# A graph network's second message layer: scattered rows kept in SBUF or sent through DRAM, twenty or twenty-six batches gathered beside a copy

## What is computed

```python
deg = maximum(segment_sum(ones, dst), 1)            # per node
s = deg ** -0.5
h = relu(layernorm(x))
x = x + s * segment_sum((s * h)[dst] * edge_weight, src)          # layer 0
h = relu(layernorm(x))
x_i, x_j = h[dst], h[src]
feat = concat([x_i, x_j - x_i])                                    # 512 wide
msg = relu(feat @ W1 + b1) @ W2 + b2                               # 512 -> 512 -> 256
x = x + segment_sum(msg, dst) / (segment_sum(ones, dst) + 1e-8)    # layer 1
```

## Time and profile before

| | |
|---|---|
| median of 3 timed runs | 2128.58 us (2127.1 to 2130.37) |
| the profiled execution | 2115.95 us, span of its core 2114.1 us |
| mean granted TensorE clock | 0.914 |
| busy, share of the span | TensorE 80%, VectorE 69%, ScalarE 48%, GpSimd 60% |
| DMA | 376.43 MB |

### The profile page before, as it was taken

One profiled execution on the slowest core, in us unless ns is written; L12 is line 12 of the kernel. 1 busy time (PEld: TensorE's weight loads), 2 busy tenths in 40 slices (PEclk: granted clock), 3 DMA queues, 4 the chain that ended last, 5 costly groups with the idle time before them and its releaser, 6 DMA issues.

```text
span 2114.1 us, 45720 instructions
## 1 busy us (share of the span) xinstructions
PE 1692.6 (80%) x13740; PEld 1478.0 (70%) x13740; DVE 1465.7 (69%) x5883; ACT 1009.9 (48%) x2064; POOL 1261.7 (60%) x1004
## 2 busy tenths in 40 slices
PE   4958888887676676620599999999999999999991
PEld 1238877776576566620488889888888888888881
DVE  6969989897677666720477777777767767677660
ACT  0014445443333333310376666767666656666561
POOL 2023323268888878865443433378888888888854
PEclk9979999998888888865799999999999999999996
DMA  7989999856565565545999999955555555555543
GB/s 242 318 295 336 323 334 326 270 103 107 99 109 103 98 105 101 102 50 94 335 326 333 342 336 339 336 114 97 95 94 92 97 94 97 92 97 94 95 65 39
DMA packets 140468, 376.43 MB, mean 178 GB/s; under 512 B 31392, under 2 KB 95657, under 8 KB 127529
## 3 DMA queue, kind: packets, MB, share of 16 engines
q0 software_dynamic: 84672, 128.51, 33.9%
q1 hardware_dynamic: 27452, 208.63, 27.4%
q10 hardware_dynamic: 28304, 38.85, 7.0%
HBM read 323.36 MB, written 258.12 MB: 275 GB/s over the span
## 4 chain that ended last, share of the span: by engine, by line
POOL 21%; PE 18%; issue 11%; DMA 3%; ACT 0%; DVE 0%; ACTq 0%; POOLq 0%; DVEq 0%
POOL table_out L937 11%; POOL ends L925 10%; PE ps_h L1249 10%; PE ps_m L1263 5%; DMA table_out<-e_ring,e_targets_all 2%; PE ps_t L1236 2%; PE ps_s L1276 2%; ACT ends L1148 0%; DMA ends<-x,keys 0%; DVE e_moments L999 0%; ACT hid L1162 0%; DVE out_sum L1071 0%; ACTq L1133 0%; POOLq L935 0%; DVE out_lo L1076 0%
## 5 line engine op out<-in xcount | busy, mean ns | idle before, releaser
L925 POOL DMA_INDIRECT ends<-x,keys x392 | 399.3, 1019 | 306.9 <-PE ps_h L1249 109.0
L774 PE MATMUL ps_deg<-table,hot 128*128 128x128 bf16 x5488 | 352.9, 226 | 80.4 <-issue 72.6
L774 PEld LDWEIGHTS ps_deg<-table,hot 128*128 128x128 bf16 x5488 | 328.7, 101 | 99.7 <-issue 91.0
L467 POOL DMA_INDIRECT x<-sums_ring,targets_all x196 | 323.4, 1650 | 89.0 <-issue 63.5
L937 POOL DMA_INDIRECT table_out<-e_ring,e_targets_all x196 | 319.9, 1632 | 92.2 <-issue 55.9
L457 POOL DMA_INDIRECT rows<-in_x,row_idx x196 | 205.1, 1046 | 240.9 <-ACT normed L702 188.3
L1249 PE MATMUL ps_h<-feat_hi,w_hi 128*128 128x512 f32 x784 | 314.2, 401 | 9.4 <-DVE feat_lo L1066 4.8
L1249 PE MATMUL ps_h<-feat_lo,w_hi 128*128 128x512 f32 x784 | 310.4, 396 | 0.0
L1249 PE MATMUL ps_h<-feat_hi,w_lo 128*128 128x512 f32 x784 | 310.3, 396 | 0.0
L788 PE MATMUL ps_sum<-msg_hi,same 128*128 128x260 f32 x784 | 151.0, 322 | 137.7 <-issue 131.2
L1263 PE MATMUL ps_m<-w_hi,hid_hi 128*128 128x256 f32 x784 | 227.9, 291 | 9.8 <-DVE hid_lo L1061 8.3
(11 more groups left out here) (141 smaller groups left out, 3447.2 us busy)
## 6 DMA issues: line engine op xcount, KB each, us to landing
table_out<-x SPq DMA_DIRECT2D x400, 252.0 KB
x<-in_x SPq DMA_DIRECT2D x400, 250.0 KB
hi_row<-hi_rows ACTq DMA_DIRECT2D x49, 256.0 KB
src_row<-src_rows ACTq DMA_DIRECT2D x49, 256.0 KB
dst_row<-dst_rows ACTq DMA_DIRECT2D x49, 256.0 KB
ends<-x,keys POOLq DMA_INDIRECT x392
rows<-in_x,row_idx POOLq DMA_INDIRECT x196
x<-sums_ring,targets_all POOLq DMA_INDIRECT x196
```

Of the source, the lines that this page charges most:

```text
L467: pool.indirect_dma_start(out=x1_d, out_offset=bass.IndirectOffsetOnAxis(ap=targets_all[:, b, j:j + 1], axis=0), in_=sums_ring[:, b % RING ...
L774: last = nc.tensor.matmul(ps_deg[q][k][:, j * P:(j + 1) * P], hot[:, c, k, j * P:(j + 1) * P], table[:, c, part, :], start=(c == 0 and par ...
L925: pool.indirect_dma_start(out=ends[b % NE][:, n, :], out_offset=None, in_=x1_d, in_offset=bass.IndirectOffsetOnAxis(ap=keys[:, 1 - end, at ...
```

## The change

`e_ring` goes. ScalarE's `scale` writes into one of two tiles `e_sums`, and a new `keep(b, q)` at the end of ScalarE's step writes the batch, half a megabyte, to `sums_d` in DRAM. SP, once it has issued the copy, reads the batches back in order into six tiles `back`, and `scatter` reads from those; `e_in_ring` is now `e_scaled`, and `e_ring_free` is `back_free`, for which SP waits and not ScalarE. The space goes to the gathers: NE is 10 and LEAD1 is 26. The pace of the lead is a new one: its batches 2 to 25 are spread over TensorE's steps 0 to 15. After the copy 9/4 gathers go with each half batch. The loops of the three compute engines are written out.

```diff
     RING0 = 26
-    RING1 = 20
-    NE = 4
+    BACK = 6
+    NE = 10
     LEAD0 = 24
-    LEAD1 = 20
+    LEAD1 = 26
+    sums_d = nc.dram_tensor("sums_d", (NB, P, W * D), fp32).ap()
...
-            e_ring = sb("e_ring", [P, RING1, W, D], fp32)
+            e_sums = [sb(f"e_sums{q}", [P, W, D], fp32) for q in range(2)]
+            back = [sb(f"back{k}", [P, W, D], fp32) for k in range(BACK)]
...
# SyncE, behind the copy
+                for b in range(NB):
+                    sp.wait_ge(kept[b % 2], 16 * (b // 2 + 1))
+                    if b >= BACK:
+                        sp.wait_ge(back_free, b - BACK + 1)
+                    sp.dma_start(back[b % BACK][:].rearrange("p j d -> p (j d)"), sums_d[b, :, :])\
+                        .then_inc(back_in[b % BACK], 16)
...
# GpSimd, scatter and scatter_end
-                    pool.wait_ge(e_in_ring, GROUPS * (b + 1) + g + 1)
                     if g == 0:
+                        pool.wait_ge(back_in[b % BACK], 16 * (b // BACK + 1))
                         pool.wait_ge(e_target_ready, b + 1)
...
-                            in_=e_ring[:, b % RING1, j, :], in_offset=None, compute_op=ALU.add)\
+                            in_=back[b % BACK][:, j, :], in_offset=None, compute_op=ALU.add)\
...
-                        pool.sem_inc(e_ring_free, 1)
+                        pool.sem_inc(back_free, 1)
...
# GpSimd, pace
+                STEPS = 4 * (LEAD1 - NE)
+                PAIRS = W * (LEAD1 - 2)
...
-                    elif b >= 3:
-                        if n < 4:
-                            pool.wait_ge(mm1_done, KH * (b - 3) + 2 + n)
-                        else:
-                            pool.wait_ge(mm2_done, GROUPS * (b - 3) + n // 2 - 1)
+                    elif b >= 2:
+                        step = (W * (b - 2) + n // 2) * STEPS // PAIRS
+                        c, k = step // 4, step % 4
+                        if k < 2:
+                            pool.wait_ge(mm1_done, KH * c + 2 * k + 2)
+                        else:
+                            pool.wait_ge(mm2_done, GROUPS * c + k - 1)
...
-                    for n in range(min(left, 11 * c // 4), min(left, 11 * (c + 1) // 4)):
+                    for n in range(min(left, 9 * c // 4), min(left, 9 * (c + 1) // 4)):
...
# ScalarE
+                def keep(b, q):
+                    act.wait_ge(e_scaled, GROUPS * (b + 2))
+                    act.dma_start(sums_d[bass.ds(b, 1), :, :].rearrange("o p w -> (o p) w"),
+                                  e_sums[q][:].rearrange("p j d -> p (j d)")).then_inc(kept[q], 16)
+
+                def scale(b, t, q, g):
                     act.wait_ge(e_summed, GROUPS * (b + 1) + g + 1)
-                    act.wait_ge(e_ring_free, b + 1)
+                    if g == 0 and not (isinstance(b, int) and b < 2):
+                        act.wait_ge(kept[q], 16 * t)
...
+                    if not first(b):
+                        keep(b - 1, 1 - q)
                     if load:
                         load_keys(b + 2, q)
...
# the three compute engines
-                step(*whole(0))
-                with act.Fori(0, QUADS) as i:
-                    for n in range(1, NE + 1):
-                        step(NE * i + n, 2 * i + n // 2, n % 2, n % NE, i + n // NE)
-                for b in range(NE * QUADS + 1, NB):
+                for b in range(NB):
                     step(*whole(b), last=b == NB - 1, load=b < NB - 2)
```

More of the change, by code:

```diff
@@ L882, in gnn_preln_two_layers @@
             e_summed = sem("e_summed")
-            e_in_ring = sem("e_in_ring")
-            e_ring_free = sem("e_ring_free")
+            e_scaled = sem("e_scaled")
+            kept = [sem(f"kept{q}") for q in range(2)]
+            back_in = [sem(f"back_in{k}") for k in range(BACK)]
+            back_free = sem("back_free")
             e_scattered = sem("e_scattered")
@@ L952, in pace @@
                         pool.wait_ge(ends_in[0], 16 * 2 * W)
[L953 to L957, removed]
-                        else:
-                            pool.wait_ge(mm1_done, 1)
-                    elif b >= 3:
-                        if n < 4:
-                            pool.wait_ge(mm1_done, KH * (b - 3) + 2 + n)
-                        else:
-                            pool.wait_ge(mm2_done, GROUPS * (b - 3) + n // 2 - 1)
+                    elif b == 2 and n == 0:
+                        pool.wait_ge(ends_in[1], 16 * 2 * W)
+                    elif b >= 2:
[3 more added lines that the diff above has]
+                            pool.wait_ge(mm1_done, KH * c + 2 * k + 2)
+                        else:
+                            pool.wait_ge(mm2_done, GROUPS * c + k - 1)
                 for b in range(LEAD1):
@@ L1040, in after_of @@
                     dve.wait_ge(e_deg_done, b + 1)
-                    dve.wait_ge(e_in_ring, GROUPS * b)
+                    dve.wait_ge(e_scaled, GROUPS * b)
                     nc.vector.reciprocal(inv_deg[q][:], deg_eps[:]).then_inc(inv_deg_done, 1)
@@ L1127, in _ @@
                 act.sem_inc(e_normed_done, 2)
-                act.sem_inc(e_in_ring, GROUPS)
+                act.sem_inc(e_scaled, GROUPS)
                 def load_keys(b, q):
@@ L1170, in out_high @@
                                          ACT.Copy).then_inc(out_hi_done, 1)
-                def scale(b, q, g):
+                def keep(b, q):
[3 more added lines that the diff above has]
+                def scale(b, t, q, g):
                     act.wait_ge(e_summed, GROUPS * (b + 1) + g + 1)
-                    act.wait_ge(e_ring_free, b + 1)
+                    if g == 0 and not (isinstance(b, int) and b < 2):
+                        act.wait_ge(kept[q], 16 * t)
                     act.wait_ge(inv_deg_done, b + 1)
-                    act.sem_inc(waited, 1)
                     for a in range(G):
                         j = G * g + a
-                        last = nc.scalar.activation(e_ring[:, bass.ds(b % RING1, 1), j, :], ps_s[g][:, a * D:(a + 1) * D],
+                        last = nc.scalar.activation(e_sums[q][:, j, :], ps_s[g][:, a * D:(a + 1) * D],
                                                     ACT.Copy, scale=inv_deg[q][:, j:j + 1])
-                    last.then_inc(e_in_ring, 1)
+                    last.then_inc(e_scaled, 1)
                 def step(b, t, q, u, v, last=False, load=True):
@@ L1202, in step @@
                         if not first(b):
-                            scale(b - 1, 1 - q, g)
+                            scale(b - 1, t - 1 + q, 1 - q, g)
                         out_high(b, g)
+                    if not first(b):
+                        keep(b - 1, 1 - q)
                     if load:
@@ L1213, in _ @@
                     feat_high(0, k)
-                step(*whole(0))
-                with act.Fori(0, QUADS) as i:
-                    for n in range(1, NE + 1):
-                        step(NE * i + n, 2 * i + n // 2, n % 2, n % NE, i + n // NE)
-                for b in range(NE * QUADS + 1, NB):
+                for b in range(NB):
                     step(*whole(b), last=b == NB - 1, load=b < NB - 2)
                 for g in range(GROUPS):
-                    scale(NB - 1, (NB - 1) % 2, g)
+                    scale(NB - 1, (NB - 1) // 2, (NB - 1) % 2, g)
+                keep(NB - 1, (NB - 1) % 2)
             @block.tensor
@@ L1270, in sums @@
                         pe.wait_ge(out_lo_done, GROUPS * b + g + 1)
-                        pe.wait_ge(e_in_ring, GROUPS * b + g + 1)
+                        pe.wait_ge(e_scaled, GROUPS * b + g + 1)
                         for a in range(G):
```

3 lines of the change are left out of this document (removed).

## The result

The changed kernel takes 2142.73 us (median of 12 runs, 2134.51 to 2146.03), the kernel before 2127.84 us in the same sessions: ratio 1.0068, 95% interval 1.0056 to 1.0080. It is slower by 15 us; the forecast was 12.4 us slower. The profiled execution has a span of 2138.9 us.

A forecast was written before the change was run, and what follows sets the result against it. GpSimd's scatters and gathers bound the kernel: first scatter at 1435.5, plus 576 with gathers, 109 without and 6, gave a 2126.5 us span, 12.4 more than before, so 2141 timed; range 2107 to 2175.

The forecast's parts named there:

- What sets the end: Layer 1: GpSimd's scatters and gathers set the end; TensorE keeps 34 us in hand.
- The copy's end: Layer 1 during the copy: added traffic lengthens it by 52 us (bounds 27 and 64); first scatter 50 us later.
- The gathers' share: During the copy: 53 more gathers, 6.9 MB at 3.5 us per MB; with row loads 27 us.
- The writes': During the copy: writing 9.2 MB of kept sums to DRAM adds 26 to 37 us.
- Rival A: During the copy: added traffic is cheap, 27 us not 52, giving 2116; faster if under 35 us; chance 0.29.
- The rhythm: After the copy: groups with gathers take 7.05 us each (bounds 6.92 and 7.4), 81.75 groups making 576 us.
- Rival B: After the copy: scatters wait for reads and writes, 7.4 and 7.5 us a group, giving 2183; chance 0.10.
- Groups without gathers: Last scatters: 6.7 us a group instead of 6.28 (bounds 6.28 and 7.5), 16.25 groups making 109 us.
- The sum: Whole kernel: 1435.5 + 576 + 109 + 6 = 2126.5 us of span, 12.4 more than before; 2141 timed.
- The small terms: Extra DMA issue, buffers, tiles, unrolled loops and a start effect: covered; unrolling gives at most 0.4 us per iteration.
- Batch 2's late gathers: Layer 1's start: VectorE waits for them, so TensorE loses some 10 us once, with 34 us still in hand.
- That TensorE stays at 20.47 us: Layer 1: TensorE's batches keep 20.47 us each, with one gap of about 10 us in step 0.

The follow-up runs named there:

- the repeat: The changed kernel itself run again, on the third chip beside three others; ratio 1.0066 to the kernel before.
- DRAM alone: Changed kernel with 20 batches beside the copy, 4 ends tiles, old pace and 11/4 gathers a group, keeping the messages' way through DRAM; ratio 1.0215.
- reads alone: Changed kernel without writes to DRAM; SP reads as many bytes from x1 instead; ratio 0.9864 on the second chip, 0.9937 on the third.
- the halves: Changed kernel with every write and read cut in two of 0.26 MB, same bytes; ratio 1.0014 on the second chip, 1.0080 on the third.
- no trip: Changed kernel without the messages' write to DRAM and read back, scatters adding zeros; ratio 0.9908, and 0.9890 in the second session.
- loops out: Kernel before with the loops of the three compute engines written out, nothing else changed; ratio 1.0011.
- six ends: Two kernels: the one before, loops written out, 16 ring places, 6 ends tiles, 22 batches ahead; ratio 0.9926 with 5/2 gathers a group, 1.0015 with 11/4.
- writes alone: Changed kernel with the writes to DRAM but without SP's reads, scatters adding zeros; ratio 0.9988.
- the four repeats: Third-chip reruns: changed kernel 1.0066, without DRAM writes and reads 0.9890, with reads only (from x1) 0.9937, with transfers cut in two 1.0080.

## Why the prediction was right, and its sizes

**What sets the end.** Right. GpSimd's chain of scatters does, before and after; TensorE's last sums stand 53 us ahead of the last scatter.

**The copy's end.** The mechanism was right: GpSimd stands for 40 us, the engines are at 0.98 until then. The term was 50 us and measured 41.5 (44.4 in the repeat). The gathers' share was right on the first chip, where it was measured alone: 21.7 us for 48 gathers, 6.3 MB, which at my 3.5 us per MB are 22. The writes' was the one that was mis-sized. I priced a written MB at 2.8 to 4.0 us, like rows of other queues; 9 MB cost 12.6 to 16.3 us on the first chip, and on the third 14.6 by the last copy DMA, not 26 to 37. The 3 us for the first read back are borne out: from the last copy DMA to the first scatter pass 8.8 and 10.2 us with the trip, 5.9 and 5.8 without. Rival A was nearer on the price of a write, but the whole stayed above its point of decision (35 us).

**The rhythm.** I took 7.05 and it was 7.23: 82 groups make this 15 us. I had split it as 6.92 undisturbed and 0.13 for the trip. The undisturbed one is 7.11 and 7.12 in two kernels without a trip; the trip adds 0.11. So the trip's part was right and the price of the shorter groups was too low: late landings, nearly absent behind 2.75 gathers (0.3 us in all in the earlier trace rows), come to light behind two, mostly beside a row load, and the gathers themselves took 3% longer. The trace of before had the size, and I took one row of it: in layer 0 the scatter behind two gathers starts after 0.58 us in that row, but after 0.66 on average in all 20 such places, seven of them above 0.7 and one at 1.41, and after 0.30 in the 20 behind three (a group scatters four tiles there). With those 0.36 us in three groups of four the sum would have been 6.88 + 0.27 = 7.15. That the trip adds so little is not general either: in the kernel with DRAM alone it added 0.29 a group (7.81 against 7.52), though more gathers stand between; why stays open. Rival B did not decide: two-gather groups took 7.04 and 7.00 us on average, under the 7.2 that I had named as the limit.

**Groups without gathers.** 6.7 expected, 6.65 measured, 6.36 and 6.43 without the trip.

**The sum.** The first scatter 8 us less, the time after the copy 14 us more (a saving of 23, not 37): +18.6 in the profiles where the sum had 12.4, and +14.9 in the timed runs. The terms missed by 8 us one way and 14 the other. That the total came within 3 us in timed runs is in part luck; the direction and the chain that sets it are not.

**The small terms.** The loops cost nothing that shows (1.0011, interval with 1). Batch 2's late gathers did stall TensorE. VectorE waits for them and comes late to its next work, and TensorE waits for that ahead of step 1's products:

```profile
1062.05 1.40 DVE L1008 BATCH_NORM_STATS2 e_moments<-ends 128x6 f32<-128x256 f32 x4 [9.21 <-DMA ends<-x,keys]
1065.97 0.79 PE L1259 MATMUL ps_h<-feat_hi,w_hi 128*128 128x512 f32 x1 [6.12 <-DVE feat_lo L1075]
```

Step 1 starts 64.5 us behind layer 1's start, 58.7 before: 6 us, not 10, and covered as forecast, since the last sums follow the last gather (2024.6) by 50 us as before. That TensorE stays at 20.47 us was wrong: its batches in the changed kernel are some 21.3 us apart beside the copy. The chain that ended last, two of its products:

```profile
1108.96 11.44 PE ps_h L1259 x48
...
1130.35 11.29 PE ps_h L1259 x48
```

With that, 0.8 us in each of 19 steps, it still was not the end.

**Where the gain went.** Moving 48 gathers ahead of the copy's end is worth 20 to 23 us by the ratios (0.9908 on the first chip, 0.9890 on the third) and 17 to 22 by the medians (2109.11 against 2125.68, 2105.5 against 2127.66). The trip that makes room for them costs 37 us. The change does what it says and pays more for the space than the space brings.

## What to carry to other kernels

Space bought by a trip through DRAM is paid with DMA time where the DMA engines are full and with landing waits where they are not: put both in the sum, and ask first whether the same space divided otherwise (here 16 ring places and 6 tiles in place of 20 and 4) gives part of the gain without a trip. Where an engine must wait for each of its transfers to land, other issues between are not only work but cover: spread them so that few waits are left bare at the end, 17 us here for the order alone (702.5 against 719.7 us behind the first scatter), and count with the collisions that a shorter cover brings to light. Before a gain is put down to an edit, look at which stretch it stands in, and repeat it beside its rival on one chip. Where a forecast leans on one row of a trace, take the mean of all rows like it.

## What the hardware showed that I had not expected

Beside a DRAM-to-DRAM copy that keeps the engines 0.98 busy, a written MB from SBUF displaced 0.41 to 0.53 MB of the copy in three pairs of profiles on two chips. A gathered MB displaced 1.01 in one pair and 0.28 and 0.53 in two others, on the second chip.

Executions on different chips differ in the copy. Reads alone had its first scatter at 401.7 us on the second chip and 413.9 on the third, the halves at 415.2 and 429.6; no trip gave 416.6 on the first and 415.2 on the third. All queues together moved 344 and 331 GB/s in the two profiles of reads alone. The ratio of one kernel moved by up to 0.007 with it (reads alone 0.9864 and 0.9937, halves 1.0014 and 1.0080). The kernel before gained nothing on the second chip (2130.82 us there, 2125.68 on the first and 2127.66 on the third). That fits its profile, where the first scatter follows the lead's last gather after 0.30 us and not the copy, but it was not profiled on that chip. So a ratio to it depends on the chip as well.

TensorE's batch takes 20.47 us with 8 gathers in it (before, loops out) and with 9 (six ends). With 12 it takes about 21.2 us in seven profiles (changed, no trip, writes alone and the four repeats) and yet 20.47 from the third batch on in two, reads alone and halves on the second chip: 259.5 and 259.1 us busy of the 260 from 1100 to 1360, against 252.4 in no trip. So it is not the number of gathers that stretches it, nor writes, nor the loops. In no trip VectorE stands 13.0 us in that window ahead of `out_sum` for something that ended outside the engines, in the two of the second chip 0. A landing that comes late is a guess; no run tried it.
